# Attention in units of two steps, with the value mixing split at 64 keys and 64 queries

## What is computed

```python
xn = _layernorm(x)
q, k, v = xn @ Wq, xn @ Wk, xn @ Wv      # 32 query heads, 8 key/value heads of 64
q, k = rope(q, k)
allowed = (j <= i) & (i - j < 128)       # causal, window of 128 keys
attn = softmax(where(allowed, q @ k.T / 8, -inf))
out = x + (attn @ v) @ Wo + ffn(xn)      # ffn: Hadamard, gate/up, silu, Hadamard, down
```

## Time and profile before

| what | value |
|---|---|
| median of 3 runs | 1434.48 us (1433.56 to 1437.24) |
| the profiled execution's own time | 1436.66 us |
| its span in the trace | 1434.6 us |
| PE busy | 1340.1 us, 93% |
| DVE, ACT, POOL busy | 900.7, 753.2, 677.1 us |
| attention of row 3 (628.97 to 755.59 us) | 126.6 us |
| FFN of the next row (755.59 to 798.57 us) | 43.0 us |

### The profile page before, as it was taken

The page is one execution under the profiler, slowest core; times in us unless marked ns, Lnnn a source line. Parts: engine busy times, 40 slices in busy tenths (PEclk is TensorE's granted clock), DMA queues, the critical chain, the costliest instruction groups (busy, mean ns, idle before and its releaser), DMA issues. The chain is left out here.

```text
span 1434.6 us, 34061 instructions
## 1 busy us (share of the span) xinstructions
PE 1340.1 (93%) x12776; PEld 1045.3 (73%) x12776; DVE 900.7 (63%) x1496; ACT 753.2 (53%) x2685; POOL 677.1 (47%) x719
## 2 busy tenths in 40 slices
PE   6889888999999999999999999999999999999998
PEld 3676666867778677877778677786777877787776
DVE  6657664467755677457773677546775477745775
ACT  2355654266643666346662666536664466634665
POOL 5225533065532665336651565416654266523664
PEclk9899989999999999999999999999999999999999
DMA  6223341423423342323424244143332234231342
GB/s 229 70 59 119 108 140 52 118 75 104 119 66 84 107 115 86 105 62 97 124 62 133 55 112 124 37 118 89 92 117 85 78 100 116 82 110 46 90 112 60
DMA packets 71554, 138.35 MB, mean 96 GB/s; under 512 B 15328, under 2 KB 29152, under 8 KB 71136
## 3 DMA queue, kind: packets, MB, share of 16 engines
q1 hardware_dynamic: 70400, 135.46, 32.6%
q10 hardware_dynamic: 992, 0.73, 0.2%
HBM read 73.21 MB, written 12.58 MB: 60 GB/s over the span
## 5 line engine op out<-in xcount | busy, mean ns | idle before, releaser
L485 POOL TENSOR_TENSOR e_sb<-e_sb,rinv 128x512 f32<-128x512 f32 x256 | 266.6, 1042 | 367.8 <-DVE rinv L830 360.3
L592 ACT ACTIVATE e_sb<-S,negmax 128x128 f32<-128x128 f32 x1024 | 363.0, 369 | 110.0 <-DVE negmax L825 108.9
L602 ACT ACTIVATE pt_sb<-TR 128x512 f32<-128x512 f32 x256 | 153.2, 599 | 174.8 <-PE TR L1048 173.9
L818 DVE COPY_PREDICATED S<-diagonal_key,S 128x512 f32<-128x512 int8 x192 | 133.1, 693 | 171.8 <-PE S L1037 169.5
L709 DVE TENSOR_TENSOR prod<-PROJ,rope_sb 128x1024 f32<-128x1024 f32 x160 | 195.0, 1219 | 64.3 <-PE PROJ L895 63.4
L1037 PEld LDWEIGHTS S<-k_stack,q_stack 64*64 64x64 f32 x5632 | 172.1, 133 | 74.7 <-issue 49.5
L1048 PE MATMUL TR<-ident,e_sb 128*128 128x128 f32 x1024 | 168.8, 288 | 55.8 <-POOL e_sb L485 49.7
L1037 PE MATMUL S<-k_stack,q_stack 64*64 64x64 f32 (+2 forms) x5632 | 214.1, 276 | 0.0
L592 ACT ACTIVATION_READ_ACCUMULATOR e_sb<-S,negmax 128x1 f32 x1024 | 211.8, 207 | 0.0
L825 DVE TENSOR_REDUCE negmax<-S 128x4 f32<-128x512 f32 x256 | 176.9, 691 | 8.8
L1048 PEld LDWEIGHTS TR<-ident,e_sb 128*128 128x128 f32 x1024 | 108.6, 141 | 88.0 <-POOL e_sb L485 73.1
(11 more groups left out here) (96 smaller groups left out, 2659.8 us busy)
## 6 DMA issues: line engine op xcount, KB each, us to landing
q_stack<-qy SPq DMA_DIRECT2D x512, 64.0 KB, 2.0
wq_ring<-wq_split_d SPq DMA_DIRECT2D x56, 512.0 KB, 3.8
wo_ring<-wo_split_d SPq DMA_DIRECT2D x56, 512.0 KB, 3.9
k_stack<-ky SPq DMA_DIRECT2D x256, 64.0 KB, 3.0
x_in<-x SPq DMA_DIRECT2D x8, 512.0 KB, 4.5
wq_split_d<-wq_ring SPq DMA_DIRECT2D x8, 512.0 KB, 3.7
wo_split_d<-wo_ring SPq DMA_DIRECT2D x8, 512.0 KB, 4.3
out<-acc SPq DMA_DIRECT2D x8, 512.0 KB, 4.9
```

Source lines behind the costliest of these rows:

```text
L485: nc.gpsimd.tensor_tensor(e, e, r, ALU.mult).then_inc(norm_done, 1)
L592: last = nc.scalar.activation(e_sb[:, n % 2, r, :], s_heads(n, 1)[:, r, :], ACT.Exp, bias=negmax[:, n % 2, r:r + 1], accum_out=rowsum[:, n ...
L602: nc.scalar.activation(pt_sb[:, n % 4, :, :], TR[:, :, :], ACT.Copy).then_inc(t_copied, 1)
```

## The change

The 32 steps are run as units of two: in unit u (0 to 16) PE runs the scores of steps 2u and 2u + 1, the transposes of step 2u - 2, the fillers of slot 2u, the transposes of step 2u - 1, the fillers of slot 2u + 1 and then the mixing of both steps 2u - 2 and 2u - 1. All engines' loops, the slots of the projections and SP's order of the weight loads are rewritten to match. The mixing is now done in halves of 64 queries: V of the previous tile (for the first 64 queries) or `v_mix` (for the others: the first 64 rows of the own V tile, the last 64 of the previous one; made by DVE's new `value_mix`) times `pt_sb`, and then, only on the 64-by-64 blocks on the diagonal, `v_step` times `p_cur` in quarter-array matmuls. Steps with i = 0 have no mask and no second term. The two halves of O are in two PSUM banks, that of O and that of TR, so the transposes of an even step also wait for `o_split`. `xn` has a buffer of its own. The diff, cut to its core:

```diff
-    ROPE_SLOTS = {("q", 2, 0): (0, 1), ("q", 3, 0): (4, 5), ("q", 4, 0): (7, 8), ("k", 1, 0): (10, 11),
-                  ("q", 5, 0): (13, 14), ("q", 6, 0): (17, 18), ("q", 7, 0): (21, 22), ("k", 0, NEXT): (27, 28),
-                  ("q", 0, NEXT): (31, 32)}
-    NORM_SLOT = 24
+    UNITS = STEPS // 2 + 1
+    ROPE_SLOTS = {("q", 2, 0): (0, 1), ("q", 3, 0): (4, 5), ("q", 4, 0): (6, 8), ("k", 1, 0): (10, 12),
+                  ("q", 5, 0): (14, 16), ("q", 6, 0): (18, 20), ("q", 7, 0): (22, 24), ("k", 0, NEXT): (28, 30),
+                  ("q", 0, NEXT): (32, 33)}
+    NORM_SLOT = 25
...
+        O_half = [O[:, 0:2 * P].rearrange("p (s m q) -> p s m q", s=2, m=2),
+                  TR[:, 0:2, :].rearrange("p s (m q) -> p s m q", m=2)]
...
@@ SP, in the loop over heads n = 2 to 7 after both stacks @@
-                    if not b and 2 <= n <= 6:
-                        save_wq(n + 1)
-                    if 2 <= n <= 4:
-                        load_wq(b, n + 3)
-                    if 5 <= n <= 6 and b + 1 < BATCH:
-                        load_wq(b + 1, n - 5)
                     if n >= 3:
                         if not b and n >= 5:
                             save_wo(n - 3)
                         load_wo(b, n - 1)
+                    m = {2: 5, 3: 6, 5: 7}.get(n)
+                    if m:
+                        if not b:
+                            save_wq(m - 2)
+                        load_wq(b, m)
+                    if n >= 6:
+                        if not b:
+                            save_wq(n)
+                        if b + 1 < BATCH:
+                            load_wq(b + 1, n - 6)
@@ POOL @@
+                for u in range(UNITS):
+                    if u:
+                        normalise(2 * u - 1)
+                    for n in (2 * u - 2, 2 * u - 1):
+                        for kind, m, row in rope_jobs(b, n, 1):
+                            rotate(row, kind, m)
+                    for n in (2 * u - 2, 2 * u - 1):
+                        if n >= 0 and n % TT:
+                            mask(n)
+                    if u < UNITS - 1:
+                        normalise(2 * u)
+                    if u < TT - 1:
+                        value_step(u + 1)
+                for n in (2 * UNITS - 2, 2 * UNITS - 1):
                     for kind, m, row in rope_jobs(b, n, 1):
                         rotate(row, kind, m)
@@ ACT @@
-                    nc.scalar.activation(o_p[0][:, :, i * P:(i + 2) * P],
-                                         O[:, :].rearrange("p (m q) -> p m q", m=2), ACT.Copy
-                                         ).then_inc(o_copied, 1)
+                    for a in range(2):
+                        last = nc.scalar.activation(o_half(0, i, a), O_half[a].rearrange("p s m q -> p m s q"), ACT.Copy)
+                    last.then_inc(o_copied, 1)
...
+                for u in range(UNITS):
+                    if u:
+                        t_copy(2 * u - 2)
+                    if u < UNITS - 1:
+                        exps(2 * u)
+                    read_fillers(2 * u)
+                    if u:
+                        t_copy(2 * u - 1)
+                    if u < UNITS - 1:
+                        exps(2 * u + 1)
...
+                    read_fillers(2 * u + 1)
+                    if u:
+                        o_copy(u - 1)
@@ DVE (o_low is cut in two halves as o_copy is) @@
+                def value_mix(i):
+                    dve.wait_ge(v_done, b * TT + i + 1)
+                    HP = P // 2
+                    nc.vector.tensor_copy(v_mix[0:HP, i - 1, :], v_sb[0:HP, i, :])
+                    nc.vector.tensor_copy(v_mix[HP:P, i - 1, :], v_sb[HP:P, i - 1, :]).then_inc(v_mixed, 1)
+                for u in range(UNITS):
+                    if u:
+                        inverse_sum(2 * u - 1)
+                    if u >= 2:
+                        o_low(b, u - 2)
+                    if u < UNITS - 1:
+                        fold(2 * u)
+                        fold(2 * u + 1)
+                    if u < TT - 1:
+                        value_mix(u + 1)
+                    if u < UNITS - 1:
+                        inverse_sum(2 * u)
+                    for n in (2 * u, 2 * u + 1):
...
+                        for kind, row, m, part in fillers(b, n):
...
@@ PE @@
+                    if n >= 2 and n % 2 == 0:
+                        pe.wait_ge(o_split, (b * STEPS + n) // 2)
                     for r in range(REP):
                         last = nc.tensor.transpose(TR[:, r, :], e_sb[:, n % 2, r, :], ident[:, :])
...
+                def values_mixed(pair):
+                    HP = P // 2
+                    pe.wait_ge(t_copied, b * STEPS + 2 * pair + 2)
+                    pe.wait_ge(v_done, b * TT + min(2 * pair + 2, TT))
+                    pe.wait_ge(v_mixed, b * (TT - 1) + min(2 * pair + 1, TT - 1))
+                    if pair:
+                        pe.wait_ge(o_split, b * STEPS // 2 + pair)
+                    for s in range(2):
+                        g, i = divmod(2 * pair + s, TT)
+                        heads = slice(g * D, (g + 1) * D)
+                        for a in range(2):
+                            v = v_mix[:, i - 1, heads] if i and a else v_sb[:, max(i - 1, 0), heads]
+                            for odd in range(2):
+                                last = nc.tensor.matmul(O_half[a][odd * D:(odd + 1) * D, s, :, :], v,
+                                                        pt_sb[:, (2 * pair + s) % 4, odd:REP:2, a * HP:(a + 1) * HP],
+                                                        start=s == 0, stop=False)
+                    pe.wait_ge(v_stepped, b * (TT - 1) + min(2 * pair + 1, TT - 1))
+                    for s in range(2):
...
+                        if i:
+                            pe.wait_ge(p_masked, b * MASKS + masks_upto(2 * pair + s))
+                            for odd in range(2):
+                                for a in range(2):
+                                    half = slice(a * HP, (a + 1) * HP)
+                                    last = nc.tensor.matmul(O_half[a][odd * D:(odd + 1) * D, s, :, :],
+                                                            v_step[half, i - 1, heads], p_cur[half, (2 * pair + s) % 4, odd:REP:2, half],
+                                                            start=False, stop=s == 1)
+                    last.then_inc(pv_done, 2)
...
+                for u in range(UNITS):
+                    if u < UNITS - 1:
+                        scores(2 * u)
+                        scores(2 * u + 1)
+                    if u:
+                        transposes(2 * u - 2)
+                    fill(2 * u)
+                    if u:
+                        transposes(2 * u - 1)
+                    fill(2 * u + 1)
+                    if u:
+                        values_mixed(u - 1)
```

More of the change, by code:

```diff
@@ L114, in attention_and_ffn_block @@
         USES += [("v", b, 0, 0), ("v", b, 0, 1)]
-        for n in range(LAST_SLOT + 1):
+        for n in range(2 * UNITS):
             USES += fillers(b, n)
@@ L123, in place, with masks_upto @@
         return TURN[what] % 2, TURN[what] + 1
+    def masks_upto(n):
+        return n - n // TT
+    MASKS = masks_upto(STEPS - 1)
     def stacked(b, g, semaphores, each):
@@ L177, in attention_and_ffn_block @@
         v_step = sb("v_step", [P, TT - 1, NKV * D])
-        staging_rest = sb("staging_rest", [P, CT * 2 * F - (TT - 1) * NKV * D])
+        v_mix = sb("v_mix", [P, TT - 1, NKV * D])
+        staging_rest = sb("staging_rest", [P, CT * 2 * F - 2 * (TT - 1) * NKV * D])
         qy = sb("qy", [P, 2, 2, T])
@@ L190, in attention_and_ffn_block @@
         p_cur = sb("p_cur", [P, 4, REP, P])
+        xn = sb("xn", [P, TT, C])
         scale_d_b = sb("scale_d_b", [P, C])
@@ L206, in attention_and_ffn_block, with o_half @@
         O = ctx.enter_context(nc.psum_tensor("O", [P, 512], fp32))
+        O_half = [O[:, 0:2 * P].rearrange("p (s m q) -> p s m q", s=2, m=2),
+                  TR[:, 0:2, :].rearrange("p s (m q) -> p s m q", m=2)]
         PROJ = ctx.enter_context(nc.psum_tensor("PROJ", [P, 2, 512], fp32))
         S4 = S[:, :, :, :, :].rearrange("p a b h k -> p (a b) (h k)")
+        def o_half(part, i, a):
+            tokens = o_p[part][:, :, i * P:(i + 2) * P].rearrange("p m (s a q) -> p m s a q", s=2, a=2)
+            return tokens[:, :, :, a, :]
         def s_heads(n, which):
@@ L279, in attention_and_ffn_block @@
         v_stepped = sem("v_stepped")
+        v_mixed = sem("v_mixed")
         pv_done = sem("pv_done")
@@ L636, in _, with read_fillers @@
                 v_copy(1)
-                for n in range(LAST_SLOT + 1):
+                def read_fillers(n):
                     for kind, row, m, part in fillers(b, n):
@@ L641, in _ @@
                             v_copy(part)
-                        elif kind == "x" and part == 0:
+                        elif kind == "x":
```

(38 more changed lines are left out.)

7 lines of the change are left out of this document (1 added, 6 removed).

## The result

The changed kernel takes 1507.6 us (median, 1499.74 to 1509.71), the kernel before 1435.9 us on the same chip. The ratio is 1.0489, with a 95% interval of 1.0453 to 1.0525. The forecast was 1503 us. The profiled execution has a span of 1508.0 us, 73.4 more than before.

A forecast was written before the change was run, and what follows sets the result against it. PE was taken to bound attention. A row: 15.1 + 100.1 + 1.6 + 0.55 + 10.95 + 6.8 = 135.1 us for 126.6; eight rows add 68 us to 1436.66, less 2.2 to the median: 1503 us, range 1456 to 1560.

The forecast's parts named there:

- The start: Row's beginning: transposes of step 2 start at about 15.1 us for 13.2 before; mixing in unit 2 waits some 1.6 us.
- The unit: Each two-step unit: reading O joins the chain, giving a period of 7.15 us, not 6.57 by PE's work alone.
- The mixing: PE's mixing of a pair: 1.61 us (i = 2, 3) or 1.40 (i = 0, 1), on average 1.50 for 1.66.
- third rival: Base term of the mixing: weight loads lie open, 8 a pair at 138 ns, 141 us more, 1644 us; chance 0.05.
- The stacks: Scores of steps 20, 24, 28: late q stacks make PE wait 2.9 us; 3.65 us each with slow clock, 10.95 a row.
- The k stack: k1, rotated in unit 7 and needed in unit 8: lands at 8.1 us, 0.55 us lost a row.
- second rival: PE's first scores in units 8, 10, 12, 14: stacks land in time, 1411 us, faster than before; chance 0.12.
- The clock: Behind each of three stack waits a row: slower PE clock costs 1.4 us more, bounds 0 and 2.4.
- first rival: At the stack waits: the clock stays up, 34 us less than forecast, 1469 us; chance 0.20.
- The end: Row's end, from transposes of step 30: 6.8 us for 7.6 before.
- the 14 units: The units of a row between start and end: 100.1 us for 105.8 before.
- Row 0, taken as the others: First row's attention: own waits for weights ignored, counted like every row as 8.5 us more.

The follow-up runs named there:

- slots' run: Changed kernel with projection slots from the second part of q4 on one unit earlier, so heads rotate in units 8, 10, 12: 1434.9 us, 0.9989 to before.
- run with PE kept busy: Changed kernel with ten overwritten matmuls of 512 columns put before the stack waits of steps 20 and 24: 1487.9 us, ratio to before 1.0377.

## Why the prediction was right

By its own steps, in row 3:

- **The start.** Forecast 15.1 us to the transposes of step 2, measured 14.2 (648.97 to 663.14), for 13.2 before. The wait for `v_step` in unit 2 was 1.45 us for 1.6.
- **The unit.** Forecast 7.15 us, measured 7.06. The two halves of `o_copy` start 0.28 us apart and take 0.66 us together for the 0.83 of the forecast; `o_low` was as taken. The waits are 0.57 and 0.33 us. The runs with the old mixing confirm the cause: without the shared bank the wait is gone.
- **The mixing.** Forecast 1.61 and 1.40 us, which include 0.15 for the pipeline's end; measured from start to start 1.51 and 1.29. The weight loads are hidden: 16 instructions in 1.02 us are 64 ns each, with a load of 138 ns for each in the earlier trace rows and 137 to 140 in the new trace. So the third rival falls. What lets them overlap here, no run tells.
- **The stacks.** Forecast waits of 2.9 us at three heads, measured 3.27, 2.50 and 1.20 in row 3 and 2.86 on average over all rows. The third, behind the long unit with the next row's input, varies most, from 0.90 to 3.38 us in the inner rows; why was not traced. For the forecast of 11.5 us a row, the units around them are 10.8 us longer than 6.95 and 7.17 us in an inner row. The slots' run puts the price at 9.8 there (9.1 over all rows), with new waits of its own in it. The k stack cost little: 0.17 us of waiting in row 3, but 1.38 in row 1 and 1.76 in row 0, for 0.55 forecast. The second rival, that they land in time, is what the slots' run made true: 1434.9 us, where the rival had 1411. The unit with the next row's input, 3.5 us longer than the others in that run in 7 rows, is as large as the difference; its other gains and losses nearly cancel.
- **The clock.** Forecast 1.4 us a stack. The stretch behind the 24 waits took 1.4 us more than its 3.15 on average, by 0 to 2.7 us; the net gain of the run with PE kept busy was 1.2 at each of two. The first rival falls. That a value read from one place of the kernel before met the average of so wide a spread is luck in part.
- **The end.** Forecast 6.8 us from the transposes of step 30, measured 6.8 in row 3 (776.39 to 783.23) and in rows 0 and 1, but 8.2 to 8.4 in rows 2, 4, 5 and 6. The wait ahead of these transposes is the same in all of them, 2.29 to 2.31 us; only the clock behind it differs, here in rows 3 and 4:

```profile
776.39:778.39 2.00, 2.00 (x12) 1.68 (x13) 0.00 (x0) 0.60 (x1) 1.46 (x2) 1.00 0.02 4
956.49:958.49 2.00, 2.00 (x7) 1.81 (x8) 0.00 (x0) 0.60 (x1) 1.00 (x2) 0.50 0.00 0
```

Some terms were left out, one was too large and one assumption failed; they nearly cancel. The unit with the next row's input takes 11.0 us for 7.1 in row 3 with the third stack's wait in it, and 10.6 without one in the slots' run: both transposes are followed at once by a filler that needs their bank, which waits 1.95 us for `xt_lo`, and that filler then runs slow:

```profile
754.55 0.58 PE L938 MATMUL PROJ<-wo_ring,o_hi 128*128 128x256 f32 x1 [1.95 <-DVE xt_lo L696]
754.93 0.42 PE L939 MATMUL PROJ<-wo_ring,o_hi 128*128 128x256 f32 x1
755.14 0.41 PE L940 MATMUL PROJ<-wo_ring,o_lo 128*128 128x256 f32 x1
```

Here 0.21 us lie between the matmuls for 0.12, at a granted clock of 0.51 (754.55 to 756.50). Before the transposes of step 30 the wait is 2.29 us, which no scores cover, so that the unit takes 7.6 us for 7.15, with the slow clock of four rows behind it, 1.5 us each. Some 0.6 us of the wait comes from a table load that ACT has ahead of `o_copy` in that unit only (row 7, which has none there, waits 1.66 us):

```profile
773.42 1.28 ACT L561 ACT_TABLE_LOAD   x1
774.71 0.20 ACT L561 ACTIVATE spare<-ident 128x1 f32<-128x1 f32 x1
774.82 0.37 ACT L634 ACTIVATE o_hi<-O 128x256 fp32r<-128x256 f32 x1
```

In an inner row these make 3.5, 0.5 and on average 1.0 us. Against them the stacks were taken 0.7 us too dear, the start 0.9 and the 14 units 1.3. So the six inner rows are 10.7 us longer, not 8.5. Row 0, taken as the others, is 1.3 us shorter. Four waits of 2.2 to 3.3 us for POOL's `e_sb`, which it had before (the earlier trace rows has two of them), are gone there, and the stacks cost it only 4.8 us; why they went was not traced. Six rows at 10.7, one at 11.7 and one at -1.3 make 74.6 us; the span grew by 73.4. That 1503 came within 5 us of 1507.6 is partly this luck.

## What to carry to other kernels

When a stage is regrouped, follow each buffer from its last writer to its first reader on every queue: here a rotation moved back by one unit met 8 DMA issues of 0.62 to 0.69 us each (row 3) and left some 3 us of idle PE at three places a row, with a slow clock behind; moving it forward again won 73 us. The cheaper matmuls, whose output takes a bank on the critical path, cost more here than they saved: 0.27 us of mixing a unit (1.40 for 1.66 on average) was bought with waits of 0.45 and, once a row, 2.3 us. And a gain ahead of a late transfer counted only in part here: the old mixing gave 26 us with the stacks late and 34 with them in time. So mend the transfer first.

## What was not expected of the hardware

- The same wait costs differently from row to row, because the clock does not fall behind each. After an idle stretch of 2.50 us the scores ran at a granted clock of 0.61 (740.50 to 742.40); behind 3.27 us they still ran at 0.94 (722.74 to 724.00), and only then came 3.3 us at 0.50 (724.05 to 727.30). Row 7 waited 2.52 and 3.18 us and needed 3.15 us for the stretch behind each, at a granted clock of 1.00 (1442.42 to 1445.58 and 1459.34 to 1462.49). Ahead of the transposes of step 30 waits of 2.29 to 2.31 us were followed by 1.00 in three rows and by 0.50 in four. So the length of the wait alone does not tell; what else does stays open.
- Ten superfluous matmuls of 512 columns at two places a row made the kernel 20 us faster (1507.6 to 1487.9).
- One ACT table load of 1.28 us delays PE by some 0.6 us once a row (a wait of 2.29 us in row 3, of 1.66 in row 7 without the load), since it lies ahead of the reading of O. In the kernel before a load of the same length just ahead of the same transposes (747.91 in row 3) cost PE nothing: the transposes started at 747.99 without a wait.
